# Gate and up values with features on partitions: two block transposes on VectorE in place of TensorE transposes

## The reference, cut to what matters

```
xn = layernorm(x)                                   # (2, 4096, 512)
def fp4_quant_dequant(x):                           # blocks of 16 along the last dimension
    scale = max(max(|block|) / 6, 1e-12)
    q = GRID[searchsorted(MID, |block / scale|)] * sign * scale
def fp4_linear(x, w):  return einsum('bsk,nk->bsn', fp4_quant_dequant(x), fp4_quant_dequant(w))
gate = fp4_linear(xn, w_gate)                       # 512 -> 1408
y    = fp4_linear(xn, w_up)                         # 512 -> 1408
h    = silu(gate) * y
ffn  = fp4_linear(h, w_down)                        # 1408 -> 512
out  = x + attn(xn) + ffn
```

## Time and profile before

| | |
|---|---|
| median of three executions | 3267.94 us |
| profiled execution | 3265.77 us, its span 3263.9 us |
| mean granted TensorE clock | 0.998 |
| TensorE matmul busy | 3167.7 us, 97% |
| VectorE busy | 1874.0 us, 57% |
| ScalarE busy | 992.7 us, 30% |
| GpSimd busy | 862.4 us, 26% |

### The profile page before, as it was taken

The page is one execution under the profiler, slowest core; times in us unless marked ns, Lnnn a source line. Parts: engine busy times, 40 slices in busy tenths (PEclk is TensorE's granted clock), DMA queues, the critical chain, the costliest instruction groups (busy, mean ns, idle before and its releaser), DMA issues.

```text
span 3263.9 us, 45150 instructions
## 1 busy us (share of the span) xinstructions
PE 3167.7 (97%) x16324; PEld 2624.8 (80%) x16324; DVE 1874.0 (57%) x4413; ACT 992.7 (30%) x1758; POOL 862.4 (26%) x918
## 2 busy tenths in 40 slices
PE   2799999999999999999999999999999999999999
PEld 1588888888888888888887888888888888888887
DVE  8877777668886555555568654444444444444442
ACT  3454555532222333333332322121221222111121
POOL 7533333333333333333334111110111111110100
PEclk9999999999999999999999999999999999999999
DMA  4212122116653555555532522222222222222210
GB/s 113 69 59 77 55 83 73 39 54 155 153 142 77 134 138 134 135 135 140 132 96 47 139 49 52 43 52 36 52 52 46 52 43 52 43 52 46 49 22 24
DMA packets 585934, 256.50 MB, mean 79 GB/s; under 512 B 424049, under 2 KB 515441, under 8 KB 583153
## 3 DMA queue, kind: packets, MB, share of 16 engines
q1 hardware_dynamic: 585712, 253.62, 32.1%
HBM read 177.50 MB, written 76.05 MB: 78 GB/s over the span
## 4 chain that ended last, share of the span: by engine, by line
PE 91%; DVE 4%; issue 2%; POOL 2%; ACT 1%; DMA 0%; SPq 0%; ACTq 0%; POOLq 0%; DVEq 0%
PE bank L600 27%; PE bank L740 22%; PE bank L725 21%; PE bank L615 14%; PE bank L585 3%; PE bank L657 2%; PE bank L665 1%; POOL qa L1342 1%; PE bank L708 1%; DVE qs L833 1%; PE bank L640 1%; DVE qa L850 1%; DVE qb L858 0%; DVE HT L865 0%; POOL qa L1336 0%
## 5 line engine op out<-in xcount | busy, mean ns | idle before, releaser
L725 PE MATMUL bank<-hT,Wp 128*128 128x512 f32 x3072 | 749.2, 393 | 0.0
L740 PE MATMUL bank<-Wp,G 128*128 128x512 f32 x3072 | 743.5, 391 | 0.0
L740 PEld LDWEIGHTS bank<-Wp,G 128*128 128x128 f32 x3072 | 576.7, 188 | 125.5
L725 PEld LDWEIGHTS bank<-hT,Wp 128*128 128x128 f32 x3072 | 572.1, 188 | 120.7
L1067 DVE CAST G<-gf 128x512 fp32r<-128x512 f32 x256 | 111.2, 434 | 747.8 <-PE bank L740 746.6
L600 PE MATMUL bank<-Wu,XT 128*128 128x512 f32 (+1 forms) x2304 | 536.4, 381 | 0.0
L615 PE MATMUL bank<-Wd,HT 128*128 128x512 f32 x2112 | 523.9, 396 | 9.4 <-DVE HT L865 9.4
L600 PE MATMUL bank<-Wg,XT 128*128 128x512 f32 (+1 forms) x2304 | 525.8, 376 | 0.0
L1342 POOL TENSOR_TENSOR qa<-qb,qs 128x512 f32<-128x512 f32 (+1 forms) x290 | 318.0, 1096 | 753.7 <-DVE qb L858 750.8
L600 PEld LDWEIGHTS bank<-Wg,XT 128*128 128x128 f32 x2304 | 420.1, 188 | 68.4 <-issue 6.3
L615 PEld LDWEIGHTS bank<-Wd,HT 128*128 128x128 f32 x2112 | 391.9, 189 | 102.5 <-issue 12.3
(11 more groups left out here) (96 smaller groups left out, 2558.1 us busy)
## 6 DMA issues: line engine op xcount, KB each, us to landing
px<-in_L_attn_x_dram SPq DMA_DIRECT2D x128, 256.0 KB, 3.0
sT<-r_K SPq DMA_DIRECT2D x128, 256.0 KB, 4.1
xin<-in_L_attn_x_dram SPq DMA_DIRECT2D x66, 256.0 KB, 3.2
r_Z<-xin SPq DMA_DIRECT2D x64, 256.0 KB, 2.1
r_U<-ub SPq DMA_DIRECT2D x16, 1024.0 KB, 6.6
sU<-r_U SPq DMA_DIRECT2D x32, 512.0 KB, 4.3
r_Y<-sY SPq DMA_DIRECT2D x16, 1024.0 KB, 5.5
xl<-in_L_attn_x_dram SPq DMA_DIRECT2D x64, 256.0 KB, 3.0
```

The source lines that it names most:

```text
L725: ins = e.matmul(bk[:], Wp[f][wh][:, 0, k * P:(k + 1) * P], hT[xh][b % 2][:, k, :], start=(k == 0 and p_ == 0), stop=(k == KD - 1 and p_ = ...
L740: ins = e.matmul(ACC[j][:], G2[gh][:, n % 2, j * P:(j + 1) * P], Wp[f][wh][:, 1, :], start=(f == 0 and p_ == 0), stop=(f == 15 and p_ == 2))
```

## The change

Gate and up are computed with features on partitions: a 128-feature part of the weights is the stationary operand, and up to 512 tokens (two pairs of tiles) move past it. The two pairs in work are LAG = 3 windows apart, and each takes 11 windows, one for each 128 features, so there are NW = 179 windows; in the first three and the last three only one pair is in work and the moving operand is 256 wide. h_mult writes over the silu result sg. One VectorE instruction then transposes each 32x32 block of it into qa, which puts the features of a token side by side within a block. The quantization runs there, and a second block transpose (`h_back`) gives hq with features on partitions. ScalarE makes the high part from hq (`h_high`), and GpSimd the low part (`h_low`). TensorE transposes only weights and x. The x jobs now normalize straight into qa, and the buffer src is gone.

Gate and up have one PSUM bank each, and four banks hold the outputs of four tiles. The magnitudes always lie in qb. In the windows of the state-space matmuls, x jobs are transposed into the gate bank. The head has 49 jobs (34 w, 6 x, 9 h) in the order of ORDER, and TensorE runs gate and up of ten windows and down of eight in it, in pieces counted by PACE. Taps are in two windows of three from K0 = 13, u writes from 64, the state-space matmuls from S0 = 99. The residual is loaded a second time into its own slots. Eight of the MLP's weight pieces are prepared in the last windows.

```diff
-GB, UB_, TRB, DNB, SSB = [bank[0], bank[2]], [bank[1], bank[3]], [bank[5], bank[7]], bank[6], [bank[4], bank[7]]
-VB, BB = bank[7], bank[4]
+GB, UB_, DNB, SSB = bank[0], bank[1], [bank[i] for i in (2, 3, 5, 6)], [bank[4], bank[7]]
+VB, TRB = bank[7], [bank[4], bank[7]]
...
+def first(n): return NF * (n // 2) + LAG * (n % 2)
+def last(n): return first(n) + NF - 1
+def pairs(w): return sorted((n for n in range(NP) if first(n) <= w <= last(n)), key=lambda n: n % 3)
+ORDER = "DDWWDDXWWXXWXWDDWWWWWHDHDWHXXHWWHWWHDDWHDWHWWDWWH"
+XFRONT = {NF * i + o: 4 * i + j for i in range(1, NB) for o, j in ((-1, 2), (0, 3))}
+XFRONT.update({NF * i + o: 4 * i + j for i in range(2, NB) for o, j in ((-6, 0), (-3, 1))})
+def tap_pair(n): return 4 * (n // 3) + 2 * (n % 3) if 0 <= n < 48 and n % 3 < 2 else None
...
 def magnitudes(m):
-    return BB[:, 0:n] if m < MSSM else qb[:, m % 2, 0:n]
+    return qb[:, m % 2, 0:job_width(m)]
...
-    def h_mult(s):
-        m, n = JOF["h", s], CW[s % 3]
-        e.wait_ge(s_sg, s + 1)
-        e.wait_ge(s_gu, s + 1)
-        e.wait_ge(s_pa, m - 1)
-        e.tensor_tensor(src[:, m % 2, 0:n], UB_[s % 2][:, 0:n], sg[:, 0:n], ALU.mult).then_inc(s_src, 1)
+    def h_mult(w):
+        e.wait_ge(s_sg, w + 1)
+        e.wait_ge(s_gu, w + 1)
+        e.tensor_tensor(sg[:, 0:n], UB_[:, 0:n], sg[:, 0:n], ALU.mult).then_inc(s_hm, 1)
+        wait_qa(e, m)
+        e.wait_ge(s_hm, w + 1)
+        e.transpose(qa[:, m % 3, 0:n], sg[:, 0:n]).then_inc(s_src, 1)
+    def h_back(w):
+        e.wait_ge(s_ph, m + 1)
+        if w:
+            e.wait_ge(s_hl, w)
+        e.transpose(hq[:, 0:n], qa[:, m % 3, 0:n]).then_inc(s_t2, 1)
...
+    def h_high(w):                                  # ScalarE
+        e.wait_ge(s_t2, w + 1)
+        if w >= 2:
+            e.wait_ge(s_dn, w - 1)
+        e.activation(HT[0][:, w % 2, 0:n], hq[:, 0:n], ACT.Copy).then_inc(s_hh, 1)
+    def h_low(w):                                   # GpSimd
+        e.wait_ge(s_hh, w + 1)
+        e.tensor_tensor(lo, hq[:, 0:n], hi.bitcast(F32), ALU.subtract).then_inc(s_hl, 1)
...
     def gu_half(w, bi, part=range(KD)):             # TensorE
-            e.wait_ge(s_lo, max(TPOS[JOF["x", i]], TPOS[WLAST]))
-            if s >= 2:
-                e.wait_ge(s_src, NSOURCE[JOF["h", s - 2]])
-        ins = e.matmul(bk[:, 0:n], XT[xh][:, i % 2, k, :], W[wh][:, k, :], ...
+            e.wait_ge(s_lo, max(TPOS[m] for m in needs))
+            if w >= 1:
+                e.wait_ge((s_sg, s_hm)[bi], w)
+        ins = e.matmul(bk[:, 0:n], W[wh][:, k, :], inputs(xh, w, k), ...
...
     def window(s):                                  # VectorE
+        h_mult(s - 1)
+        front(h)
+        if low_x is not None:
+            low(low_x)
         ...                                         # scans, z_add, statistics or u writes, tile preparation
+        if fronted is not None:
+            mid_a(fronted)
+            mid_b(fronted)
+        mid_a(h)
+        mid_b(h)
         if x_ is not None:
             x_norm(...)
             front(x_)
+        h_back(s - 1)
...
     def window(s):                                  # ScalarE
-        silu(s), then high, magnitude(h), high, kernel_heads, kernel_v, kernel_taps
+        high(x_job(s - 2)), h_high(s - 2), magnitude(h_job(s)), kernel_heads, kernel_v, kernel_taps, silu(s)
         ...                                         # ssm_inputs, magnitude(x_), ssm_result
...
     def window(s):                                  # GpSimd
+        h_low(s - 2)
+        scaled(h)
         ...                                         # masks, dequant(fronted), dequant(h), kernel_sum, scaled(x_)
...
     def window(s):                                  # TensorE
+        gu_half(s, 0)
+        gu_half(s, 1)
         ssm_outputs(k // 2)
+        if x_job(s - 1) is not None:
+            turn(x_job(s - 1))
         down(s - 2)
         ssm_states(k // 2)
         kernel_turn(j)
         kernel_turn(j + 1)
```

More of the change, by code:

```diff
@@ L207, in piece @@
             Wp[f] = [high, sbt(mctx, f"Wp{f}_1", [P, 2, D], F32R)]
-        for f in range(9, 14):
+        for f in range(11, 16):
             piece(f)
@@ L212, in build @@
         yl1 = sbt(mctx, "yl1", [P, D])
-        for f in range(9):
+        for f in (8, 9, 10, 0, 1, 2, 3, 4, 5, 6, 7):
             piece(f)
@@ L688, in window @@
                     ssm_states(k // 2)
[L689 to L690 removed]
+                j = tap_pair(s - K0 - 1)
+                if j is not None:
                     kernel_turn(j)
@@ L1007, in window @@
                     mid_b(fronted)
-                if h is not None:
-                    mid_a(h)
-                    mid_b(h)
-                if s != NSTEP:
-                    for m in turns(s)[1:]:
-                        low(m)
+                mid_a(h)
+                mid_b(h)
                 if s in (K0 - 2, K0 - 1):
@@ L1098, in vector_program @@
                     inverse(m)
+                if 1 <= m <= NJ:
+                    mid_a(m - 1)
+                    mid_b(m - 1)
                 if m == 0:
@@ L1101, in vector_program @@
                     stats(1)
-                if 1 <= m <= NJ:
-                    mid_a(m - 1)
-                    mid_b(m - 1)
-            for s in range(NSTEP + 1):
+                if 20 <= m < 24:
+                    stats(m - 16)
+                if m == 23:
+                    todo.extend(batch_rsqrt(1))
+                for step in todo[0:3]:
+                    step()
+                del todo[0:3]
+            for s in range(SW, NW + 1):
                 window(s)
@@ L1428, in gpsimd_program @@
                     dequant(m - 1)
-            for s in range(NSTEP + 2):
-                if s <= NSTEP:
-                    window(s)
-                if PRE0 <= s <= NSTEP and (s - PRE0) // 3 < 4:
+                if m >= 2 and HEAD[m - 2][0] == "h":
+                    h_low(HEAD[m - 2][1])
+            for s in range(SW, NW + 1):
+                window(s)
+                if s >= PRE0 and (s - PRE0) // 3 < 4:
                     prepare((s - PRE0) // 3, (s - PRE0) % 3)
+            h_low(NW - 1)
             for n in range(2, 16 * NB + 2):
```

501 lines of the change are left out of this document (256 added, 245 removed).

## The result

The changed kernel takes 3370.62 us (median of four executions, 3368.86 to 3373.64), the kernel before 3268.52 beside it: ratio 1.0315, 95% interval 1.0297 to 1.0333. That is +102 us; the prediction had +10 and a range that ended at 3330. The profiled execution of after has a span of 3371.8 us.

The account below looks back on a forecast made before the run. TensorE, busy 97%, bounds the kernel before; VectorE's chain and the loops bind parts of the changed one. Terms -50 + 26 + 31 - 5 + 5 = +7, say +10, gave 3276 us profiled, median 3278, range 3222 to 3330.

Parts of the forecast that it names:

- TensorE's side: TensorE's savings: about 700 transposes beyond the head at 0.09 us, -63 us; gate and up matmuls, -10 us.
- the price of the block transpose: VectorE's transpose of an h job: 0.69 us, 0.72 where the next instruction waits; range 0.43 to 1.0.
- the dearer weight job: Head: VectorE and GpSimd exclude each other once magnitudes are in SBUF, so a job takes about 3.8 us against 3.1.
- the silu loop: Windows with taps: silu, h_mult, magnitude and taps form a one-window loop of 9.2 us, 10.25 with the kernel_v copy.
- u-write windows: Windows 64 to 95: VectorE's chain exceeds TensorE's time by 0.8 us a window, +26 us in 32.
- Rivals 1 and 2: First: TensorE stays the bound, full case 3218 us, chance 0.32. Second: block transpose takes 1.0 us, 3327 us, chance 0.13.
- Rival 3: Single gate and up banks make TensorE wait, 0.3 us in each of 169 windows: 3268 us, chance 0.09.
- taps ... +31 us: Windows 13 to 60: three windows take 27.65 us against TensorE's 25.7, +31 us in all.
- SSM windows: TensorE has longer windows there ... so +0: State-space windows: no loss, as TensorE's windows are longer and VectorE's busy digits lowest there.
- the head ends "214": Head of 49 jobs: the stretch up to the last weight job's low part takes 214 us, against 136 before.
- Last 15 windows ... +5: Final windows: eight pairs of w_low and four tile preparations cost about +5 us after the slack.
- h_low "0": GpSimd's low part of h, 1.06 us, falls beside VectorE instructions without two SBUF tensors, so costs 0.

Follow-up runs that it names:

- e7: The kernel before, transposing only one 128-column part of each h job behind the head (result not the reference's): 3226.08 us, 0.9871.
- e4: The changed kernel with the magnitudes of the head's first 34 jobs in PSUM bank 6 instead of SBUF: 3354.26 us, 1.0265.
- e1: The changed kernel with silu ahead of kernel_v and the taps in ScalarE's window: 3350.48 us, 1.0252.
- e3: The changed kernel with the magnitudes of the h jobs of windows 62 to 97 in PSUM bank 7: 3363.41 us, 1.0291.
- e2: The changed kernel with the next x tile's load issued at the start of SyncE's window: 3356.91 us, 1.0273.
- e10: The changed kernel with the preparation of the MLP's input tiles and weight low parts one window later: 3367.38 us, 1.0306.
- e18: e17 with GpSimd's low part of h behind the scaling of the next job, and one more wait before the magnitudes in bank 7: 3260.26 us.
- e17: Changed kernel with e1 to e5, e9, e10, an earlier high part of x in state-space windows, and x normalized on ScalarE from window 62: 3271.59 us.
- e6: The changed kernel without the first block transpose, h_mult writing qa directly (values quantized in the wrong order): 3325.44 us, 1.0176.
- e5: The changed kernel with h_back behind the next window's h_mult instead of at the end of its own window: 3396.6 us, 1.0389.
- e9: The changed kernel with TensorE's turn of x behind down, outside the state-space windows: 3368.42 us, 1.0308.

## Why the prediction was wrong

**Right.** TensorE's side (-63 for the transposes, 58 by e7's price), the price of the block transpose, the dearer weight job and its cause (e4), the silu loop as a mechanism (e1), and the sign. The u-write windows came out (307.2 predicted, 307.8 measured), and e3 bears out their x conflict; that the sum fits to 0.6 us is in part luck, since it holds nothing for the scale instruction beside h_low. Rivals 1 and 2 fell: TensorE is not 99% busy, and the transpose is not 1.0 us. Rival 3 fell too: its wait, gate for silu, is 19.0 us in the head and 19.9 us from there to 700 us, where the taps are, and 0.6 us in all that follows. Two slips in the prediction carry nothing: VectorE's tenths are 6 in some slices before 1000 us, and the 3345 us for a transpose of 1.24 us would be by the second rival's working, which gives some 3365.

**Wrong: "taps ... +31 us".** The mechanism was right, the size was off. The term priced the loop with 0.45 us of x work for three windows. Three windows without x took 27.8 us where the terms without x work give 27.2; those with x took mostly 29 to 31 us. Measured, the loss is 461.2 - 48 x 8.55 = 51 us. e1 gives back 18 of it there, and what e1 leaves stands in the windows with x jobs.

**Wrong: "SSM windows: TensorE has longer windows there ... so +0".** Measured +25, of which e2 gives back 16.5. The sum had no term for the loads of the x jobs. Such a load stands at the end of SyncE's window, behind the state-space loads, whose buffers must be free, and behind the store of y, which waits for ssm_result. Two of them come late, by 11.3 us together. TensorE is the bound in these windows, so the wait is paid in full, and then again at half clock. For the gate bank the prediction had 0 to +7; gate's wait for x is 13.8 us once the loads are early.

**Wrong: the head ends "214".** 227.5. The weight job was right to 0.06 us. The first 18 low parts, all ahead of the first h job, are done where the terms put them (the last starts at 86.3 us, against about 84). The rest, with all nine h jobs, takes 141 us against about 130, so most of the excess is there; which term of an h job it is stays open. Windows 10 to 13 had no term at all: +10.5, of which e1 gives back 4.3; the rest stays open.

**Wrong: "Last 15 windows ... +5".** The stretch is 17.6 us over. e10 removed ScalarE's wait for the tile addition, and the stretch fell by 7.7. The cause of the other 10 stays open. e18's takes 139.6.

**Wrong: h_low "0".** In after the scale instruction beside it takes 281 ns in the mean and 181 alone, 23 us of VectorE's time in all. How much of that the kernel pays is not measured in after; with the loops shortened, moving h_low off it gave 11 us (e18).

**What joins them.** I summed the engines' loads and took each as hidden where another was longer. But the new kernel has one bank and one buffer where the old had two, so a late silu, load or norm reaches VectorE's next h_mult within one window, and TensorE pays it. That the lost second bank and buffer are behind this is argued and not shown: no run gives them back. Of the 102 us e1 to e4 give back 57 one by one, and all ten edits of e18 give 110. Seven of the ten are orders; e3 and e4 move magnitudes to PSUM, and e17 moves a piece of VectorE's work to ScalarE. That the block transposes need not make the kernel slower is shown by e18, which has both, all of their 238 us. With after's order and places they do cost: e6 gains 45 us by leaving out one. Which share each edit has cannot be given: alone and in company they are worth different amounts (e5 +26 and -18, e9 with e10 -5 and -17).

## What to carry to other kernels

When a change moves work to another engine and also halves the buffers, walk each loop that is now one window long, with its table loads and DMA waits in it, before summing loads; look at the slack that the lost buffer gave. Where two engines exclude each other, ask of every instruction that can fall beside the other engine's, the small ones too, and of where a moved one will land. Judge an order edit in company: one that costs time alone may pay once the loop it lengthened is gone, and one that gives nothing alone may pay when the engine behind it is on time. A VectorE that is 93% busy beside GpSimd is not proof that its work is the bound, since its waits for GpSimd are counted as busy.

## What the runs showed of the hardware

- A VectorE tensor_scalar on 128x32 elements takes 0.18 us alone and up to 1.32 us beside GpSimd's tensor_tensor of 128x512 (e5). A u write of 128x256 takes 0.54 us in the mean in e17 and 0.75 in e18, where GpSimd's low part of h runs beside it.
- The fp32 block transpose and the max reduction did not grow beside GpSimd. In all of after no block transpose of h took more than 0.717 us and no max reduction more than 0.690, although 107 of the first transposes and 193 of the reductions ran beside a GpSimd tensor_tensor.
- A fp32 block transpose of 128x512 on VectorE is 0.71 us where VectorE waited just before it and 0.65 to 0.70 directly behind another instruction, and 0.45 for 128x256.
- Behind idle time of a few microseconds TensorE's next twelve matmuls of 512 columns can be slow. In e1:

```profile
437.51 0.66 PE L638 MATMUL bank<-cs,qa 128*128 128x128 f32 x4 [2.66 <-POOL qa L1409]
...
437.92 4.58 PE L675 MATMUL bank<-Wd,HT 128*128 128x512 f32 x12
```

The group takes 4.58 us instead of 2.88, so the wait of 2.66 us cost 4.36. The granted clock is 0.50 from 438.7 to 442.0 us and 1.00 behind it. The mean granted clock is 0.978 in after, 0.987 in e18 and 0.998 before, and much of that is the head: in the first 236 us it is 0.82 in after and 0.84 in e18, and from there to 1930 us 0.98 and 1.00.
